# The begin of a decoder layer: operand waits per product, two small loads on ScalarE's queue, and the order of the first loads

## The reference, cut to what matters

```
x = layernorm(x + attention(x))         # 2 x 512 tokens, width 1024, 32 heads of 32
x = layernorm(x + quantised(x) @ quantised(ctx))
x = layernorm(x + ffn(x))               # base matrix and 8 low-rank experts, top 2

def attention(x):
    qkv = x @ qkvw + qkvb               # 1024 x 3072, bias
    scores = q k^T / sqrt(32); probs = softmax(scores); ctx = probs v
    return ctx @ ow + ob
def fake_quant(x, scale, zp):
    return (clip(round(x / scale + zp), 0, 255) - zp) * scale
```

## Time and profile before

| what | us |
|---|---|
| median of 3 runs | 720.46 (719.86 to 721.45) |
| the profiled execution | 720.5 |
| its span, first to last instruction | 718.7 |
| TensorE busy | 703.8 |
| VectorE busy | 466.2 |
| ScalarE busy | 426.5 |
| GpSimd busy | 280.9 |

### The profile page before, as it was taken

The page is one execution under the profiler, slowest core; times in us unless marked ns, Lnnn a source line. Parts: engine busy times, 40 slices in busy tenths (PEclk is TensorE's granted clock), DMA queues, the critical chain, the costliest instruction groups (busy, mean ns, idle before and its releaser), DMA issues.

```text
span 718.7 us, 11825 instructions
## 1 busy us (share of the span) xinstructions
PE 703.8 (98%) x3511; PEld 527.7 (73%) x3511; DVE 466.2 (65%) x833; ACT 426.5 (59%) x919; POOL 280.9 (39%) x206
## 2 busy tenths in 40 slices
PE   6999999999999999999999999999999999999996
PEld 5778668677686686686776866766767777888885
DVE  5887566466575574575655745557688679865574
ACT  5458668677685686776866867854467672311111
POOL 6572250171162153134135059836644834211120
PEclk9999999999999999999999999999999999999999
DMA  8757436426436335444543375745825332231101
GB/s 283 198 172 227 111 83 200 126 72 202 109 90 196 91 106 167 119 119 107 173 110 88 110 233 145 245 162 171 289 88 176 111 125 89 89 117 58 59 30 59
DMA packets 55732, 98.97 MB, mean 138 GB/s; under 512 B 10896, under 2 KB 21520, under 8 KB 54800
## 3 DMA queue, kind: packets, MB, share of 16 engines
q1 hardware_dynamic: 55408, 98.13, 44.3%
q10 hardware_dynamic: 288, 0.39, 0.2%
HBM read 56.41 MB, written 16.65 MB: 102 GB/s over the span
## 4 chain that ended last, share of the span: by engine, by line
PE 91%; issue 3%; DVE 3%; DMA 1%; ACT 0%; SPq 0%; POOL 0%; ACTq 0%; POOLq 0%; DVEq 0%
PE bank L469 58%; PE bank L595 8%; PE bank L565 8%; PE bank L609 8%; PE bank L720 4%; PE bank L746 2%; PE bank L521 1%; PE bank L735 1%; DMA kp<-k_lo 1%; DMA big_raw<-in_xT 1%; PE bank L705 1%; DVE c_raw L1376 0%; DVE m_col L1406 0%; DVE st L1480 0%; PE bank L583 0%
## 5 line engine op out<-in xcount | busy, mean ns | idle before, releaser
L878 ACT ACTIVATE probs<-bank 128x512 f32<-128x512 f32 x256 | 152.1, 596 | 119.4 <-PE bank L595 116.0
L1406 DVE TENSOR_REDUCE m_col<-bank 128x1 f32<-128x512 f32 x256 | 172.9, 687 | 77.1 <-PE bank L565 76.3
L883 ACT ACTIVATE bank<-bank,m_col 128x512 f32<-128x512 f32 x256 | 169.2, 661 | 17.7 <-DVE m_col L1406 16.1
L469 PE MATMUL bank<-big_hi,w_hi 128*128 128x512 f32 x384 | 156.9, 409 | 6.0 <-DVE big_lo L1301 5.5
L469 PE MATMUL bank<-big_lo,w_hi 128*128 128x512 f32 x384 | 152.6, 397 | 0.0
L469 PE MATMUL bank<-big_hi,w_lo 128*128 128x512 f32 x384 | 151.1, 393 | 0.0
L565 PE MATMUL bank<-kp,qp 96*128 96x512 f32 x256 | 101.5, 396 | 0.7 <-ACT bank L883 0.6
L595 PE MATMUL bank<-qp,kp 98*128 98x512 f32 x256 | 101.0, 398 | 0.0
L469 PEld LDWEIGHTS bank<-big_hi,w_hi 128*128 128x128 f32 x384 | 73.3, 191 | 25.8 <-DVE big_lo L1301 6.5
L469 PEld LDWEIGHTS bank<-big_hi,w_lo 128*128 128x128 f32 x384 | 72.8, 190 | 17.1
L469 PEld LDWEIGHTS bank<-big_lo,w_hi 128*128 128x128 f32 x384 | 73.4, 191 | 14.5
(11 more groups left out here) (141 smaller groups left out, 1108.2 us busy)
## 6 DMA issues: line engine op xcount, KB each, us to landing
w_raw<-in_wqkv SPq DMA_DIRECT2D x7, 1536.0 KB, 9.0
c_raw<-in_ctx SPq DMA_DIRECT2D x16, 512.0 KB, 3.9
qp<-q_hi SPq DMA_DIRECT2D x128, 64.0 KB, 2.0
kp<-k_hi SPq DMA_DIRECT2D x124, 64.0 KB, 2.0
big_raw<-in_xT SPq DMA_DIRECT2D x16, 256.0 KB, 5.9
qp<-q_lo SPq DMA_DIRECT2D x64, 64.0 KB, 2.0
c_scratch<-c_q SPq DMA_DIRECT2D x16, 256.0 KB, 2.2
r_all<-r_scratch SPq DMA_DIRECT2D x64, 64.0 KB, 2.0
```

Source lines behind the costliest of these rows:

```text
L469: mm = nc.tensor.matmul(dst, lhs[a], rhs[b], start=(k == 0 and n == 0) if first is None else False, stop=(k == last_k and n == 2))
L878: nc.scalar.activation(probs[:, j, t, :], bank(ST0 + i % 2), ACT.Exp).then_inc(sem["exp_ok"], 1)
L883: nc.scalar.activation(bank(max_bank(s, n)), bank(max_bank(s, n)), ACT.Exp, bias=m_col[:, n:n + 1], accum_out=l_col[:, 1 - par, n:n + 1]). ...
L1406: nc.vector.reduce_max(m_col[:, n:n + 1], bank(max_bank(s, n)), AX, negate=True).then_inc(sem["rowmax"], 1)
```

## The change

In unit 0 the six matmuls of a k are issued in another order and wait one by one; Q's high part moves from VectorE to ScalarE, K's high part of the result and its two packs of head 0 too; 36 stand-in matmuls of 128 columns run before the first product; `w_raw` has k before the piece, so that Q and K of one k are a run of 1024 bytes and V's rows runs of 512; V's weights come and are split in halves; bias and scales are loaded from ScalarE's queue; the first context tile is loaded ahead of six of the eight x loads of batch 1; the scale constants are computed behind k=1; the zeroing of `c_sum` moves between GpSimd's first splits and the fill of `kp` behind the first context tile; unit 0's tile is clipped and rounded in step 0, unit 1's clipped ahead of the last maxima; in step 1 high and low parts of q and k are made with a maximum in between; SP packs head 1's keys itself and issues the weight load of units 2 and 3 ahead of the packs of heads 2 and 3.

```
-        w_raw = at("w_raw", 88, [P, 3, KT, P], f32)
+        w_raw = at("w_raw", 88, [P, KT, 3, P], f32)
+        WV_HALVES = (slice(0, KT // 2), slice(KT // 2, KT))
+        WARM = 36
+        CONTEXT = 2
--- SP
             for k in range(KT):
-                sp.dma_start(w_raw[:, 0:2, k], wqkv[0, :, 0:2, k]).then_inc(big_in[0][k], 16)
+                sp.dma_start(w_raw[:, k, 0:2], wqkv[0, :, k, 0:2]).then_inc(big_in[0][k], 16)
                 load_x(0, k)
-                if k == 0:
-                    sp.dma_start(bias[:, :, :], qkvb).then_inc(sem["bias_in"], 16)
-            sp.dma_start(w_raw[:, 2], wqkv[0, :, 2]).then_inc(wv_in, 16)
+            for ks in WV_HALVES:
+                sp.dma_start(w_raw[:, ks, 2], wqkv[0, :, ks, 2]).then_inc(wv_in, 16)
             for k in range(KT):
+                if k == CONTEXT:
+                    sp.dma_start(c_raw[:, :], ctx_tiles[0]).then_inc(sem["ctxq_in"], 16)
                 load_x(1, k)
-            for n in range(4):
-                sp.dma_start(sc[:, n:n + 1], scales[n].rearrange("(a n) -> a n", a=1).to_broadcast([P, 1])).then_inc(sem["const_in"], 16)
...
                     wait_alone(sp, sem["lo_ok"], 2 * s + 2)
+                    if begin:
+                        pack(s, par, 1, "k")
+                        load_w()
...
                     pack(s, par, 3, "k")
-                    if begin:
-                        load_w()
--- PE
+                def first_products(k):
+                    q_dst, k_dst = bank(PROJ1), bank(PROJ0)
+                    pe.wait_ge(sem["x_hi_ok"], k + 1)
+                    pe.wait_ge(sem["wq_hi"], k + 1)
+                    nc.tensor.matmul(q_dst, w_hi[:, 0, k, :], big_hi[:, 0, k], start=(k == 0), stop=False)
+                    pe.wait_ge(sem["w_hi_ok"], k + 1)
+                    nc.tensor.matmul(k_dst, w_hi[:, 1, k, :], big_hi[:, 0, k], start=(k == 0), stop=False)
+                    pe.wait_ge(sem["x_lo_ok"], k + 1)
+                    nc.tensor.matmul(k_dst, w_hi[:, 1, k, :], big_lo[:, 0, k], start=False, stop=False)
+                    pe.wait_ge(sem["w_split"], k + 1)
+                    mm = nc.tensor.matmul(k_dst, w_lo[:, 1, k, :], big_hi[:, 0, k], start=False, stop=(k == KT - 1))
+                    if k == KT - 1:
+                        mm.then_inc(sem["proj_done"], 1)
+                    nc.tensor.matmul(q_dst, w_hi[:, 0, k, :], big_lo[:, 0, k], start=False, stop=False)
+                    pe.wait_ge(sem["wq_lo"], k + 1)
+                    mm = nc.tensor.matmul(q_dst, w_lo[:, 0, k, :], big_hi[:, 0, k], start=False, stop=(k == KT - 1))
+                    if k == KT - 1:
+                        mm.then_inc(sem["proj_done"], 1)
...
                     for k in range(KT):
-                        project(k)
-                        project(KT + k)
+                        first_products(k)
...
+            pe.wait_ge(sem["idb_ok"], 2)
+            for _ in range(WARM):
+                nc.tensor.matmul(bank(CTX, 0, P), ones16[:, :], ones16[:, :], start=True, stop=True)
             steps_of(pe, step)
--- ACT
                     nc.scalar.activation(big_hi[:, b, k], big_raw[:, b, k], ACT.Identity).then_inc(sem["x_hi_ok"], 1)
+                    if b == 0:
+                        nc.scalar.activation(w_hi[:, 0, k], w_raw[:, k, 0], ACT.Copy, scale=SM_SCALE).then_inc(sem["wq_hi"], 1)
+            act.dma_start(sc[:, 0:4], scales.rearrange("n a -> a n").to_broadcast([P, 4])).then_inc(sem["const_in"], 16)
+            act.dma_start(bias[:, :, :], qkvb).then_inc(sem["bias_in"], 16)
...
-            act.wait_ge(wv_in, 16)
-            nc.scalar.activation(w_hi[:, 2].rearrange("p k c -> p (k c)"), w_raw[:, 2].rearrange("p k c -> p (k c)"), ACT.Identity).then_inc(sem["wv_hi"], 1)
+            act.wait_ge(wv_in, 32)
+            for ks in WV_HALVES:
+                nc.scalar.activation(w_hi[:, 2, ks], w_raw[:, ks, 2], ACT.Identity).then_inc(sem["wv_hi"], 1)
...
+                if not prev:
+                    act.wait_ge(sem["proj_done"], 1)
+                    nc.scalar.activation(k_hi[:, :], bank(PROJ0), ACT.Identity, bias=bias[:, 0, 1:2]).then_inc(sem["hi_ok"], 1)
+                    act.wait_ge(sem["hi_ok"], 2)
+                    pack_first_keys(((0, k_hi), (PACK_HI2, k_hi)))
+                    split_x(1, range(2))
+                    act.wait_ge(sem["lo_ok"], 2)
+                    pack_first_keys(((PACK_LO, k_lo),))
+                    split_x(1, range(2, KT))
--- POOL
             for k in range(KT):
                 split_first_wk(k)
+                if k in (0, 2):
+                    nc.gpsimd.memset(c_sum[:, k // 2, :], 0.0).then_inc(sem["zero_sum"], 1)
+            for n, ks in enumerate(WV_HALVES):
+                pool.wait_ge(sem["wv_hi"], n + 1)
+                nc.gpsimd.tensor_tensor(w_lo[:, 2, ks], w_raw[:, ks, 2], w_hi[:, 2, ks].bitcast(f32), ALU.subtract).then_inc(sem["w_split" if n else "wv_half"], 1)
...
                     nc.gpsimd.tensor_scalar(c_raw[:, :], c_raw[:, :], sc[:, 6:7], sc[:, 3:4], ALU.mult, ALU.add).then_inc(sem["ctxq_1"], 1)
+                    if isinstance(s, int) and s == 0:
+                        pool.wait_ge(sem["ctxq_1"], 1)
+                        nc.gpsimd.memset(kp[SHIFT:SHIFT + 2, :, :, :].bitcast(f32), 1.0).then_inc(sem["plus_ok"], 1)
--- DVE
+            split_x(0, range(2))
+            quant_constants()
+            split_x(0, range(2, KT))
+            dve.wait_ge(sem["scale_q"], 1)
...
-                    if proj and n in (5, 11):
-                        low(0 if n == 5 else 1)
+                    if begin and n == 5:
+                        dve.wait_ge(sem["proj_done"], 2)
+                        low(0, ("hi",))
+                        dve.wait_ge(sem["hi_ok"], 2)
+                        low(0, ("lo",))
+                    if begin and n == 11:
+                        low(1, ("lo",))
+                    if second and n in (5, 11):
+                        low(n // 6, ("hi",))
+                    if second and n in (6, 12):
+                        low(n // 6 - 1, ("lo",))
...
                     if begin and n == 11:
                         split_x(1, range(KT))
-                    if second and n == 2:
                         clip_context(0)
-                    if second and n == 3:
                         round_context(0)
+                    if second and n == 13:
+                        clip_context(s)
-                if begin:
-                    quant_constants()
```

More of the change, by code:

```diff
@@ L307, in step @@
                         wait_alone(sp, sem["ctxq_ok"], s)
+                if proj and not (isinstance(s, int) and s == 0):
                     sp.dma_start(c_raw[:, :], ctx_tiles[bass.ds(s, 1)].rearrange("a p n -> (a p) n")).then_inc(sem["ctxq_in"], 16)
@@ L893, in step @@
                         done += 1
-                    if isinstance(s, int) and s == 0 and q in (16, 33):
-                        split_x(1, range(5) if q == 16 else range(5, KT))
-                def pack_first_keys(j):
-                    rows = slice(j * HD, (j + 1) * HD)
-                    for row, src in ((0, k_hi), (PACK_HI2, k_hi), (PACK_LO, k_lo)):
-                        act.dma_start(kp[row:row + HD, 0, j, :].bitcast(f32), src[rows, :].bitcast(f32)).then_inc(packed[j], 16)
-                if not prev:
-                    act.wait_ge(sem["lo_ok"], 2)
-                    pack_first_keys(0)
-                    pack_first_keys(1)
                 if proj:
@@ L1109, in _ @@
                 split_first_wk(k)
-            pool.wait_ge(sem["wv_hi"], 1)
-            nc.gpsimd.tensor_tensor(w_lo[:, 2], w_raw[:, 2], w_hi[:, 2].bitcast(f32), ALU.subtract).then_inc(sem["w_split"], 1)
+                if k in (0, 2):
[3 more added lines that the diff above has]
+                nc.gpsimd.tensor_tensor(w_lo[:, 2, ks], w_raw[:, ks, 2], w_hi[:, 2, ks].bitcast(f32), ALU.subtract).then_inc(sem["w_split" if n else "wv_half"], 1)
             pool.wait_ge(sem["w_split"], FIRST + 2)
-            nc.gpsimd.memset(kp[SHIFT:SHIFT + 2, :, :, :].bitcast(f32), 1.0).then_inc(sem["plus_ok"], 1)
-            pool.wait_ge(sem["plus_ok"], 1)
-            nc.gpsimd.memset(c_sum[:, :, :], 0.0).then_inc(sem["zero_sum"], 1)
-            pool.wait_ge(sem["zero_sum"], 1)
+            pool.wait_ge(sem["zero_sum"], 2)
             def add_context(s, b):
@@ L1355, in step, with low @@
                 begin = isinstance(s, int) and s == 0
[L1357 removed]
+                def low(piece, parts=("hi", "lo")):
                     hi, lo = ((q_hi, q_lo), (k_hi, k_lo))[piece]
[L1360 to L1369 removed]
+                    source = bank(PROJ1 if piece == 0 else PROJ0)
+                    column = bias[:, bass.ds(g, 1), piece:piece + 1].rearrange("p a b -> p (a b)")
+                    if "hi" in parts:
+                        wait_alone(dve, sem["proj_done"], 3 * s + piece + 1)
+                        if not isinstance(s, int) or s >= 1:
```

(12 more changed lines are left out.)

55 lines of the change are left out of this document (20 added, 35 removed).

## The result

The changed kernel takes 723.98 us, median of nine runs (722.82 to 726.62), and the kernel before, on the same chip, 721.39 (719.86 to 722.26): the ratio is 1.0049, with a 95% interval from 1.0037 to 1.0061. It is slower by 2.6 us by the medians (the ratio makes it 3.5), where 2.8 us less were forecast. The profiled execution of after took 726.62 us (span 724.8), the longest of its nine, against 720.5 (718.7) before; so its trace shows where time goes, but more of it than the median has.

What follows compares the result with a forecast made beforehand. TensorE was taken as the bound, busy 703.8 of 718.7 us. The terms 1.45 + 0.25 + 0.65 + 0.5 - 0.05 = 2.8 us came off 720.5, giving 717.7 us, range 715.9 to 719.3.

Steps and rivals of the forecast that it cites:

- the weight load, moved ahead: Load for units 2 and 3, issued near 25.3, lands by 32.3 to 34.7; no loss taken, other end 1.6 us.
- the slow rival: Packs behind the weight load make head 2's last pack land at 38 or later; 722 us, chance 0.05.
- The reading of the earlier trace under this step: In SP's queue a large load holds small transfers back: an 8 KB store behind one took 9.2 us.
- V starts at 18.0, gain 1.45: End of unit 0's Q and K products: TensorE paces k=3 onward, V's products start at 18.0, gaining 1.45 us.
- Product k=2: In unit 0, the constants moved forward add a wait of about half a microsecond; k=2 ends near 11.1.
- between V's start and the first score: Unit 1's first score no longer waits for the k_lo pack, wanted at 26.25: gain 0.25 us.
- the wait for the reciprocals: Unit 1: only rounding stays between last maximum and reciprocals, so the wait before their transpose goes: gain 0.5 us.
- the clip ahead of the maxima: Unit 1's clip moves ahead to maximum 13; GpSimd's scaled tile is there at 39, before the clip.
- The strided rows of w_raw: Units 2 to 15: strided reads priced at nothing; a tenth more on GpSimd's passes stays hidden by TensorE.
- The wait of 0.6 before score 9 goes: gain 0.65: Unit 1's scores: with q_hi and q_lo apart by a maximum, the wait before score 9 disappears, gaining 0.65 us.
- VectorE is late next … with 0 to 0.6 lost: After x_lo, clip and rounding, the first maximum starts at 27.9; score 3 just in time, 0.05 us loss taken.
- The premise: What the begin gives TensorE stays given, provided nothing later was waiting for something else.

Runs made afterwards that it cites:

- Experiment 2: The kernel before with only the weight load moved ahead of head 2's packs: 722.47 us against 720.41, ratio 1.0029.
- experiment 12: The kernel before with head 1's key packs on SP's queue and the weight load behind them, ahead of head 2's packs: 723.41 us against 720.42.
- experiment 13: The kernel of experiment 1 with unit 1's clip behind the last maximum again: 721.99 us against 720.24 for the kernel before.
- experiment 3: The changed kernel with the weight load on ScalarE's queue, behind the second x_hi: 723.30 us against 720.41 for the kernel before.
- Experiment 5: The changed kernel with the nine scale constants behind the split of k=7 instead of k=1: 722.77 us against 720.62 for the kernel before.
- experiment 1: The changed kernel with the weight load back behind head 3's packs: 725.26 us against 720.41 for the kernel before.
- Experiment 14: The same kernel as experiment 9, timed in more rounds: 720.11 us against 720.24 for the kernel before, ratio 0.9998.
- experiment 9: The changed kernel's begin only, with what follows the products as in the kernel before: 719.80 us against 720.42, ratio 0.9988.
- experiment 11: The kernel before with the 36 stand-in matmuls alone: 720.72 us against 720.42, ratio 1.0000.
- 4: The kernel of experiment 1 without the 36 stand-in matmuls: 725.64 us against 720.41 for the kernel before.
- 8: The kernel of experiment 1 with constants behind k=7, head 1's keys on ScalarE, and x_hi, q_hi, q_lo, V^T, clip and rounding reordered: 723.96 us against 720.62.
- 6: The kernel of experiment 1 with q_hi and q_lo of unit 1 behind maxima 8 and 9: 725.89 us against 720.62 for the kernel before.
- 7: The kernel of experiment 1 with head 1's three key packs issued from ScalarE's queue: 725.55 us against 720.62 for the kernel before.

## Why the prediction was wrong

**The step that failed is "the weight load, moved ahead", with its "I take no loss; the other end is 1.6".** Four things were wrong in it. The load is issued at 28.84, not 25.3, for which the prediction shows no working: the nine packs in front of it start at 21.53 and take 0.63 each, one of them 1.95. The prediction's threshold was head 2's first score at 35.1; the packs' first waiter with no slack is q_hi of unit 1 on VectorE, which wants the packs of all four heads, and which in the kernel before had them 1.7 us in hand. VectorE works in order, so its 5.0 us there became 2.4 on TensorE by way of maxima and exponentials. The wait for the k_lo pack, 1.8, is the one that the slow rival described, at the place that it named, and its condition was met: head 2's last pack landed at 38.2, and it asked for 38 or more. But it saw that only with a load of over 11 us, and this one took 7.8: the lateness came from the queue (the pack went out at 32.47, 27.25 before) and from the 5.7 us that it took beside the load. And no term had the clock: after the two waits TensorE ran eleven matmuls at 1.2 GHz, 2.2 us. Experiment 2 (2.1 us for the load alone) and experiment 12 (3.0 for load and keys) show that this step is enough for a loss of after's size. It is not the whole of it: experiment 13, with the load back and the clip back, still loses 1.8. And experiment 2 loses its 2.1 by another wait than after. The share of the keys alone was not run by itself, and the intervals of 2 and 12 overlap.

The reading of the earlier trace rows under this step, that a queue holds small transfers back behind a large one, failed too: experiments 2 and 3 have the load in one queue and the slow packs in the other, at up to 9.2 and 8.3 us.

**"V starts at 18.0, gain 1.45" failed too.** Product k=2 did wait, but until 11.24 and 1.5 us, not about a half: the constants took 2.3 us (8.11 to 10.42) instead of 1.16, because one of them stood 1.27 us beside GpSimd's memset of c_sum. I had costed that memset on GpSimd and on TensorE and not on VectorE. At the end x_lo and w_lo of k=7 took 1.77 and 1.38 instead of 0.69 and 0.29, beside GpSimd's two splits of V (15.86 to 18.89). So k=3 begins at 12.28, where the forecast had 11.1, and the last product of k=7 adds 0.3: that is the 1.4. Experiment 5 moves the constants away, and V starts at 17.71. The landings were as taken (k=1 at 6.48 for 6.5; V's weights at 14.93 for 15.0 to 15.5, 1.8 us behind k=7 where the rows gave 1.7), and so was the stride of 0.23 from the first product on in this profile.

**Right, with its size:** between V's start and the first score 0.37 was gained for 0.25, and the wait for the reciprocals went (0.5 forecast, 0.6 found). With clip and rounding at 49.83 and 52.77 for 0.68 and 0.73 us the reciprocals come at 53.43. In after itself the clip ahead of the maxima costs nothing, as argued, since the load is early enough; experiment 1 shows that it rests on this. The strided rows of w_raw, priced at nothing, did cost nothing: a split pass of GpSimd takes 1.05 and 2.3 to 2.4 us in both kernels, and its busy time is 280.2 against 280.9.

**"The wait of 0.6 before score 9 goes: gain 0.65"** failed. That score waits 2.38 in after and 1.06 in experiment 13, because q_hi, ahead of its exponential's maximum in VectorE's queue, waits for the packs.

**"VectorE is late next … with 0 to 0.6 lost":** nothing was lost at scores 3 and 4.

**The premise** that what is given in the begin stays given is the deeper fault. It holds where nothing later waits for something else, as I wrote, and I checked that for scores only. Behind unit 0's operands comes a chain of packs through SP at 0.63 us each, 18 before and 21 in after, whose end VectorE awaits. It starts from the last operand of q and k, and no step of the sum asked when that comes: with k finished first and the constants in front, q_hi is at 19.74 instead of 18.48, so the packs start 1.3 us later in a kernel whose V products start no later. Experiment 14 undoes that order and the moves behind it, head 1's keys on SP's queue among them, and is 1.9 us faster than experiment 13 by the medians. How much of this is the order of q and k, how much the three packs, how much VectorE's other moves, was not separated.

**The begin itself** is worth 0.02% and 0.12% by the ratios of experiments 14 and 9, at the edge of what is measurable, though their profiles start V 1.8 and 0.6 us earlier. Unit 1's products then meet other waits: experiment 9 has 0.6 before score 9 as before, experiment 14 0.8 before the transpose of V and 0.4 before score 9. That the time does not follow the first score is shown; where each tenth of it goes in the runs without a profile is not. After's loss in the median, 2.6, is also less than the 6.1 of its profile. Its shorter runs are not free of the low level: the mean granted clock of its nine runs is 0.992 to 0.996, 0.994 in the profiled one, and 0.997 to 0.999 in every run of the kernel before beside the experiments. Which waits are smaller in them is not shown.

## What to carry to other kernels

Before a DMA or a pack is moved in a queue, list every engine that waits for the last one behind it, buffer reuse included, and take the first of them that has no slack; count a fixed issue time for each small DMA in front, and price each at its time beside the big transfer. A long stall of TensorE is priced with the slow matmuls that may follow it, here 1.4 to 2.9 us more behind waits of 2.3 to 2.8. An operation that is moved to fill a gap on one engine must be priced against what the engine that shares its port runs there. And an edit that was tuned together with another (a clip moved ahead, a load that makes it possible) can't be undone or kept alone: test pairs. Where one issue of a DMA can take 1.4 us more in one profile than in the next, two profiles that differ by so much show nothing about the edit between them.

## What the runs showed of the hardware

**A small operation of VectorE can last as long as GpSimd's instruction beside it.** The 128x2 operation at 8.59 lasts 1.27 us and ends at 9.86, GpSimd's memset from 8.89 for 0.95 ends at 9.84; in experiment 5 a 128x1 operation at 17.60 lasts 1.20 and ends at 18.80, GpSimd's split at 18.79. In the kernel before the same two last 0.17 and 0.16. The Trainium skill (SBUF — State Buffer, Who interferes with whom) has the two engines share a port pair, for those operations of VectorE that use it, and whoever issues first holds it for a whole instruction; these rows agree with it.

**The stand-ins lift the clock only sometimes.** Of the twelve profiles with 36 stand-ins, six have the first product at the high level (duration 0.47 us) and six at the low one (0.76 to 0.80, strides of 0.43 to about 10 us), with the stand-ins from 1.13 on in both. The first product waited 0.63 to 1.05 us in the six and 0.49 to 0.95 in the others, so that doesn't tell them apart. In two of the first six the stand-ins took 3.7 us instead of 4.02. What decides it is open. The profiles of experiments 9 and 14, the same kernel, differ in it, and by 1.6 us of span; experiment 11, the stand-ins alone, gained nothing.

**Behind its longest waits TensorE ran slowly.** Each wait of a score from 2.3 to 3.3 us here (after; experiments 1, 3, 4, 5, 8, 12) was followed within 1.3 us by seven or more matmuls at the low level, with strides of 0.43, and so were the waits of 3.7 and 5.3 before the transposes in 6 and 7. After the waits of 1.0 to 1.5 in 2, 7, 8 and 13, after the 1.8 of after's score 8, and after the 2.1 before experiment 1's transposes, the strides stayed at 0.23. So the 2.5 of experiment 12 is 3.9 with the 1.4 behind it, the 2.4 of after 4.6 with its 2.2, and the 2.3 of experiment 5 is 5.2, since fourteen slow matmuls behind it cost 2.9.

**Packs of 64 KB between parts of SBUF slow down beside a large load**, 2.0 us alone, 5 to 9 beside 1.5 MB, in the load's own queue (up to 7.7 in experiment 2) as in another (9.2 there, 8.3 in experiment 3). **ScalarE's DMA issues run ahead of its activations**: the load of experiment 3 went out at 22.69, when activations in front of it in the program ran until 25.86.
